# Two steps of an attention kernel written out anew: scores ahead of the values in front, exponentials ahead of weight roundings

## What is computed

```
x = x + tanh(g_x) * MHA(layernorm(x), ctx, ctx)        # 16 heads of 16
t = layernorm(x) * rsqrt(mean square + eps) * norm_w
probs = softmax(t @ gate_w.T); the two best of 8 experts, weights normalized
h1 = t @ w1.T + 2 * (t @ a1[e].T) @ b1[e].T            # rank 16 per expert
h3 = t @ w3.T + 2 * (t @ a3[e].T) @ b3[e].T
act = silu(h1) * h3
out_e = act @ w2.T + 2 * (act @ a2[e].T) @ b2[e].T
x = x + tanh(g_f) * sum over the two experts of weight * out_e
```

## Times and profile before

| | |
|---|---|
| three runs, median (lowest to highest) | 507.07 us (504.67 to 507.3) |
| the profiled execution, its own time | 509.6 us |
| its span, first to last instruction | 507.7 us |
| busy PE / DVE / ACT / POOL | 487.7 / 357.9 / 266.6 / 282.4 us |
| mean granted TensorE clock | 0.993 |

### The profile page before, as it was taken

The page is one execution under the profiler, slowest core; times in us unless marked ns, Lnnn a source line. Parts: engine busy times, 40 slices in busy tenths (PEclk is TensorE's granted clock), DMA queues, the critical chain, the costliest instruction groups (busy, mean ns, idle before and its releaser), DMA issues.

```text
span 507.7 us, 11754 instructions
## 1 busy us (share of the span) xinstructions
PE 487.7 (96%) x4350; PEld 456.2 (90%) x4350; DVE 357.9 (70%) x768; ACT 266.6 (53%) x584; POOL 282.4 (56%) x339
## 2 busy tenths in 40 slices
PE   7888999999999999999899999999999999999996
PEld 6657999999999999997789999899999999999994
DVE  6866777877878877888577869856486456854444
ACT  4456766666676777667666533443335333233331
POOL 5645666666666666561676536644386444854440
PEclk9989999999999999999989999999999999999999
DMA  7793786677777777553601000010000100001001
GB/s 199 180 289 93 216 214 153 157 182 190 189 179 180 180 176 169 120 111 57 204 10 17 1 0 1 1 34 0 1 0 2 34 1 1 0 2 34 0 1 32
DMA packets 51144, 45.83 MB, mean 90 GB/s; under 512 B 33935, under 2 KB 40115, under 8 KB 51088
## 3 DMA queue, kind: packets, MB, share of 16 engines
q1 hardware_dynamic: 41310, 23.18, 19.6%
q0 software_dynamic: 7504, 18.69, 14.1%
q10 hardware_dynamic: 2274, 3.21, 2.0%
HBM read 20.59 MB, written 6.66 MB: 54 GB/s over the span
## 4 chain that ended last, share of the span: by engine, by line
PE 84%; DVE 6%; DMA 5%; issue 2%; ACT 2%; POOL 1%; ACTq 0%; DVEq 0%
PE bank L1368 14%; PE bank L1223 7%; PE bank L1246 7%; PE bank L1372 7%; PE bank L1385 6%; PE bank L1420 6%; PE bank L1205 6%; PE bank L1259 6%; PE bank L1193 5%; PE bank L1400 4%; DMA QS<-crow 3%; PE bank L1292 3%; PE bank L1403 2%; PE bank L1180 2%; PE bank L1335 2%
## 5 line engine op out<-in xcount | busy, mean ns | idle before, releaser
L970 DVE TENSOR_REDUCE nmax<-bank 100x1 f32<-100x361 f32 x256 | 130.0, 529 | 38.4 <-PE bank L1223 33.4
L419 POOL TENSOR_TENSOR awl<-hb,awh 128x400 fp32r<-128x400 f32 x63 | 70.2, 1114 | 109.4 <-ACT awh L627 109.4
L529 ACT ACTIVATE pt<-bank 120x400 f32<-120x400 f32 (+1 forms) x192 | 90.3, 503 | 25.8 <-PE bank L1246 12.2
L627 ACT ACTIVATE awh<-hb 128x400 fp32r<-128x400 f32 x64 | 34.5, 539 | 119.0 <-DVE hb L906 118.7
L1223 PE MATMUL bank<-KS,QS 96*100 96x362 f32 x256 | 86.9, 358 | 5.2 <-DVE nmax L970 4.8
L899 DVE TENSOR_TENSOR hb<-sil,bank 128x400 f32<-128x400 f32 x64 | 36.5, 570 | 73.7 <-PE bank L1385 37.9
L1246 PE MATMUL bank<-QS,KS 97*120 97x200 f32 (+1 forms) x384 | 66.4, 271 | 1.6 <-ACT pt L529 1.0
L1246 PEld LDWEIGHTS bank<-QS,KS 97*120 97x120 f32 (+1 forms) x384 | 60.2, 184 | 2.8 <-DMA QS<-crow 1.7
L328 POOL TENSOR_TENSOR cth<-craw,cth 128x724 fp32r<-128x724 f32 x16 | 27.7, 1729 | 63.0 <-ACT cth L475 54.8
L1223 PEld LDWEIGHTS bank<-KS,QS 96*100 96x100 f32 x256 | 41.6, 167 | 12.8 <-DVE nmax L970 7.3
L333 POOL DMA_DIRECT2D QS<-q_dram x90 | 46.0, 519 | 0.4 <-issue 0.3
(11 more groups left out here) (221 smaller groups left out, 1116.3 us busy)
## 6 DMA issues: line engine op xcount, KB each, us to landing
KS<-kn SPq DMA_DIRECT2D x128, 90.5 KB, 3.3
KS<-kn POOLq DMA_DIRECT2D x64, 90.5 KB, 3.4
craw<-ctxT POOLq DMA_DIRECT2D x14, 361.0 KB, 4.9
QS<-q_dram POOLq DMA_DIRECT2D x92, 50.0 KB, 3.6
q_dram<-qn ACTq DMA_DIRECT2D x4, 400.0 KB, 4.1
o_dram<-on SPq DMA_DIRECT2D x16, 100.0 KB
xr<-o_dram SPq DMA_DIRECT2D x16, 100.0 KB
y<-xs SPq DMA_DIRECT2D x8, 200.0 KB
```

The source lines that it names most:

```text
L419: nc.gpsimd.tensor_tensor(awl[:, g % 2, slot], hb[:, slot], awh[:, g % 2, slot].bitcast(F32), ALU.subtract).then_inc(m["p_awl"], 1)
L529: nc.scalar.activation(pt[0:TW[t], u, :], pT[u % 3][0:TW[t], 0:CS], ACT.Exp, scale=float(DH) ** -0.5).then_inc(m["act_e"], 1)
L970: nc.vector.tensor_reduce(nmax[:, h // 8, pos % 8:pos % 8 + 1], pS[h % 2][0:S, 0:T], AX.X, ALU.max, negate=True).then_inc(m["dve_s"], 1)
```

## The change

Steps 14 and 15 get texts of their own (`late_step` and `last_step`) on PE, ACT and DVE. The rest of the attention is as it was, but for conditions that are always true now.

- PE: the first two scores of batch 15 stand ahead of the values of step 13, and units 0 to 2 of batch 15 ahead of the values of step 14. In step 15 the two halves of `u_proj` are apart, output turns and projection come earlier, `index_turn` stands behind all units, `weight_turn` behind the values.
- ACT: in step 14 exponentials come without a weight rounding between them; `row_copy` and `row_send` are parted by an exponential (before, the second followed the first at once in `row_out`). Pieces 0 to 2 are rounded between `tokens_high(0, 1)` and exponential 3 of batch 15, pieces 3 to 5 behind exponentials 9 and 10, piece 6 in tile 0. The four ACT instructions of `normed_x(1, ...)` go from step 15 to tiles 0 and 1.
- DVE: the same reductions, with the two `tokens_low`, the shares and the quotient at other places.
- POOL: the bias additions (L384) of batches 12 to 15 are all done in step 13; before, three of them stood in step 15. `second_u(0, ...)` waits for both `first_u`.
- `weight_turn(0)` waits for `d_ul` and no more for the masks.

```diff
-                for b in range(i - 2, B if i == B - 1 else i - 1):
+                for b in range(i - 2, B if i == B - 3 else i - 1):
...
             def second_u(n, low):
                 pool.wait_ge(m["p_md"], n + 1)
+                if n == 0:
+                    pool.wait_ge(m["d_u0"], 2)
...
+            def late_step():
...
+                row_copy(B - 2, 1)
+                expo(B - 2, 0)
+                row_send(B - 2, 1)
...
+                expo(B - 2, 11)
+                tokens_high(0, 1)
+                w_high(0)
+
+            def last_step():
+                expo(B - 1, 0)
+                expo(B - 1, 1)
+                w_high(1)
+                expo(B - 1, 2)
+                row_copy(B - 1, 1)
...
+                nc.scalar.activation(osb[:].rearrange("p q s -> p (q s)"), pO[:, 0:CS], ACT.Copy).then_inc(m["act_o"], 1)
+                row_send(B - 1, 1)
+                w_high(2)
...
+                w_high(3)
                 halves_of_weight(0)
                 w_high(4)
...
+                if g == 0:
+                    w_high(6)
...
-                if more and f < 2 and c:
+                if more and f < 2:
                     normed_x(c + 1, 2 * f)
                     normed_x(c + 1, 2 * f + 1)
...
+            def last_step():
+                gate(0)
+                o_turn(B - 1)
+                st_unit(B - 1, 3)
+                st_unit(B - 1, 4)
+                u_half(0, 0)
+                on_turn(B - 1)
+                st_unit(B - 1, 5)
+                st_unit(B - 1, 6)
+                st_unit(B - 1, 7)
+                u_half(0, 1)
+                st_unit(B - 1, 8)
+                st_unit(B - 1, 9)
+                st_unit(B - 1, 10)
+                y_proj(B - 1)
+                st_unit(B - 1, 11)
                 index_turn(0)
+                for u in range(UN):
+                    pv_unit(B - 1, u)
                 weight_turn(0)
```

More of the change, by code:

```diff
@@ L656, in body @@
                 expo(i, 5)
-                if has_k(i):
-                    wait(act, "pe_pv", i * UN)
-                    v_out(b, 0)
-                if i == B - 2:
-                    tokens_high(0, 0)
+                wait(act, "pe_pv", i * UN)
+                v_out(b, 0)
                 expo(i, 6)
@@ L720, in last_step @@
-                normed_x(1, 3)
+                expo(B - 1, 10)
+                w_high(5)
+                expo(B - 1, 11)
                 nc.scalar.activation(warm_s[:], nmr[:, 0:1], ACT.Silu).then_inc(m["silu_ok"], 1)
-            for i in range(0, B - 1):
+            for i in range(0, B - 2):
                 body(i)
-            last_step(B - 1)
+            late_step()
+            last_step()
             act.wait_ge(m["pe_pv"], B * UN)
@@ L1043, in body @@
                 head(i + 1, 8)
-                if i == B - 2:
-                    tokens_low(0, 0)
                 head(i + 1, 9)
@@ L1051, in body @@
                 head(i + 1, 12)
-                if i == B - 2:
-                    tokens_low(0, 1)
                 head(i + 1, 13)
@@ L1071, in body, with late_step @@
                     root(0, 6)
-            def last_step(i):
+            def late_step():
+                head(B - 1, 0)
+                head(B - 1, 1)
+                head(B - 1, 2)
+                head(B - 1, 3)
+                shares(B - 2)
+                head(B - 1, 4)
+                head(B - 1, 5)
+                quotient(B - 2)
+                head(B - 1, 6)
+                head(B - 1, 7)
+                head(B - 1, 8)
+                head(B - 1, 9)
+                tokens_low(0, 0)
+                head(B - 1, 10)
+                head(B - 1, 11)
+                turned_o(B - 2)
+                head(B - 1, 12)
+                head(B - 1, 13)
+                head(B - 1, 14)
+                first_sum(B - 2)
+                head(B - 1, 15)
+                tokens_low(0, 1)
+                variance(11)
+            def last_step():
+                shares(B - 1)
                 logits(0)
+                quotient(B - 1)
                 best_two(0)
-                shares(i)
-                quotient(i)
+                turned_o(B - 1)
                 u_low(0, 0)
@@ L1081, in last_step @@
                 masks(0)
-                turned_o(i)
                 first_u(0, 0)
                 first_u(0, 1)
-                first_sum(i)
+                first_sum(B - 1)
                 weights_of_two(0)
                 variance(13)
-            for i in range(0, B - 1):
+            for i in range(0, B - 2):
                 body(i)
-            last_step(B - 1)
+            late_step()
+            last_step()
             dve.wait_ge(m["tgf_ok"], 1)
@@ L1599, in body @@
                 s_head(i + 1, 15)
+                if i == B - 3:
+                    s_head(B - 1, 0)
+                    s_head(B - 1, 1)
                 for u in range(UN):
@@ new lines, in last_step @@
+            def last_step():
+                gate(0)
+                o_turn(B - 1)
[12 more added lines that the diff above has]
+                st_unit(B - 1, 11)
+                index_turn(0)
+                for u in range(UN):
+                    pv_unit(B - 1, u)
@@ L1622, in last_step @@
                 weight_turn(0)
-                y_proj(i)
-                for u in range(UN):
-                    pv_unit(i, u)
-            for i in range(0, B - 1):
+            for i in range(0, B - 2):
                 body(i)
-            last_step(B - 1)
+            late_step()
+            last_step()
             for g in range(NC * FT):
```

220 lines of the change are left out of this document (115 added, 105 removed).

## The result

The changed kernel takes **510.59 us** (median of 16 executions, 508.28 to 514.08); the kernel before took 507.97 us in 16 executions beside it (504.67 to 509.78). The ratio is 1.0057, 95% interval 1.0037 to 1.0078: slower by 0.57%; the medians themselves lie 2.6 us (0.52%) apart. It was wrong: the time is 4.0 us above the forecast, of which 0.9 us is the starting point (507.07 us was the median of three runs, 507.97 us is that of sixteen), 0.5 us the gain that did not come, and 2.6 us the loss that came in its place.

A forecast was written before the change was run, and what follows sets the result against it. PE's waits and low clock in steps 14 and 15 allowed at most 5.0 us; then the masks' chain binds. Step 14's 1.4 us was lost by the index turn; the entry left 0.5 us: 507.07 to 506.6 us, range 503.3 to 509.4.

The forecast's parts named there:

- Scores ahead of the values: Step 14: moving two scores of batch 15 makes PE 1.1 us late but comes to nothing, within 0.1 us.
- Step 14, 1.4 us: New order inside step 14: its values end at about 244.3 instead of 245.7, 1.4 us won.
- if later than 245: Sign of error: if step 14's values end later than 245, the walk of that step is wrong.
- Unit 6 waits for the send: Step 15, first half: PE reaches unit 6 at about 248.1 and waits 1.7 us for half 1's send.
- The send lands about 1.5 us earlier: Step 15: half 1's send, behind the weight loads, lands about 1.5 us earlier, at 249.9.
- Rival 4: Send lands 1.5 us later because batch 14's `on` store shares the engines; 1.0 survives: 507.6 us, chance 0.08.
- The index turn: End of step 15: index turn at about 252.8 against 253.00, so PE's gain is gone from the masks' chain.
- The entry: Feed-forward entry: masks' chain binds; PE waits for `first_u`, `second_u` and the projection copy; 1.7 us won, then 0.6 left.
- The four waits: PE waits between 248 and 269, from unit 6 to the projection copy: 1.7, 1.2, 1.8 and 0.7 us.
- The sum, "0.5 us won": At tile 2, beginning near 273.2 where it had begun at 273.6: 0.5 us won, bounds none and 5.0.
- Rival 3, the clock: PE's four waits lower the clock; two 3 us stretches behind tile 1 cost 3.0 us: 509.6 us, chance 0.10.

The follow-up runs named there:

- e1: Changed kernel run again, unedited, with a trace at full clock between step 13's projection and tile 3: 509.9 us, ratio 1.0057 to the kernel before.
- e12: Kernel before, unedited, one execution traced with the clock full from before step 13 to tile 3: 506.24 us.
- e8: Kernel before, unedited, one execution traced, with a low clock between step 13's projection and tile 3: 507.33 us.
- e2: Changed kernel plus 18, 9 and 8 filler transposes ahead of unit 6, the first delta and y_proj(16): 509.29 us, ratio 1.0028 to the kernel before.
- e3: Changed kernel with SP's six loads of second weight halves held until batch 15's half 1 send has landed: 506.44 us, ratio 0.9982 to the kernel before.
- e13: Changed kernel plus only the 18 filler transposes ahead of unit 6: 508.97 us, ratio 1.0034 to the kernel before.
- e9: Changed kernel with loads held, u's projection ahead of unit 5, index turn behind unit 7, roundings and tx moved: 504.59 us, ratio 0.9943 to the kernel before.
- e6: Changed kernel's new step 14 with the old order of step 15: 507.79 us, ratio 0.9999 to the kernel before.
- e11: Changed kernel, unedited, one execution traced: 509.03 us.

## Why the prediction was wrong

**Scores ahead of the values: right.** PE 1.1 us late was forecast; the values start 2.59 us behind the projection (226.81 and 229.40 above), where it was 1.28: 1.3 us.

**Step 14, 1.4 us: right in kind, 0.55 us too much.** The forecast was the end of the values, 244.3 for 245.7, or 15.2 of the ruler for 16.6. They end at 15.75: 0.85 us won. That the gate comes 1.5 us earlier, 15.8 for 17.3, is this and the 0.7 us of units 0 to 2, which stood between the two and now stand in front. The bound "if later than 245" (15.9) was just kept. The send is issued at 16.4, 0.7 us earlier than before and not 1.3, and PE comes to unit 6 at 19.7, not 19.0.

**Unit 6 waits for the send: right in kind, 1.3 us too early.** The wait of 1.7 us was forecast; it is 1.9 to 2.5 us. The forecast put unit 6 at 249.9, which is 20.8 of the ruler; e1 has 22.1. "The send lands about 1.5 us earlier" was argued from the store of `on`, the loads behind it and the send behind the loads. SP's queue of the changed kernel:

```profile
234.57 0.28 SPq L287 DMA_DIRECT2D o_dram<-on  x1
238.25 0.28 SPq L294 DMA_DIRECT2D xr<-o_dram  x1
...
241.54 0.94 SPq L301 DMA_DIRECT2D w<-w2T  x1
245.42 0.31 SPq L287 DMA_DIRECT2D o_dram<-on  x1
```

The store is at 7.76 of the ruler, 1.3 us earlier than before's 9.07, but `xr` only at 11.44 against 12.46: the loads came 1.0 us earlier, not 1.5. By as much came the send, from 23.1 (e12, where PE waits for it) to 22.1. The other 0.8 us are the landing before, which I took as 251.4, or 22.3, from a trace in which PE waited there for an exponential and did not show it; where PE does wait for it, it is 22.75 (e8) and 23.1. It moves from one execution to the next, in the changed kernel from 21.6 to 22.3. Rival 4, the store of the next `on` (the last row) sharing the engines, was given 0.08: that store now comes 2.2 us behind the send's issue, and in e12 it came 4.0 behind. But from issue to unit 6 it is 5.2 to 5.8 us in the seven traces of the changed kernel and 5.6 and 6.0 in e8 and e12, so the store has not made the send slower. From the issue of the first load to unit 6 it is 9.9 to 10.5 us in the seven and 9.9 and 10.3 in the two: the send goes out with the tail of the loads, in either order.

Here the Trainium skill had been put against the row (DMA: Bandwidth & Descriptors, "Queues, rings and completion order"). No trace agrees with a send that takes its turn: in all seven of the changed kernel its packets moved 3.3 to 5.6 us behind the issue.

**The index turn, "252.8 against 253.00 before": failed.** 252.8 is 23.7 of the ruler; it came at 25.4 in e1, 26.5 as profiled. From unit 6 on the forecast's 2.9 us of PE work became 3.3 at full clock, and 4.8 to 4.9 where the clock fell; in the old order the index turn stood 0.8 us behind unit 6 (e12). So the masks' chain, said to be no later, is 1.2 to 1.7 us later than before's 23.9 even at full clock. **This is the step that failed**, the late send and the longer walk behind it, 1.4 us together at the least (25.1 for 23.7); and all but 0.3 us of the slowdown at full clock is there already.

**The entry: right in every wait, again with sizes.** `first_u` sat out POOL as foreseen in e1 (1.69 us, beneath b3's low part); in the changed kernel as profiled, where the masks came later, the first takes 0.99 us. Then `md` starts just behind the first `first_u`, and the second just before `md` ends, and each is the longer for it. The changed kernel as profiled, DVE:

```profile
254.27 1.17 DVE L896 TENSOR_SCALAR mk<-bank,erow 128x400 f32<-128x400 f32 x2 [2.32 <-PE bank L1384]
255.48 0.99 DVE L902 TENSOR_TENSOR uth<-uTh,mk 128x800 fp32r<-128x800 f32 x1
256.38 1.83 DVE L902 TENSOR_TENSOR utl<-uTl,mk 128x800 fp32r<-128x800 f32 x1
...
264.31 2.19 DVE L918 TENSOR_TENSOR hb<-hb,wbT 128x400 f32<-128x400 f32 x1
266.53 1.30 DVE L924 TENSOR_TENSOR aws<-hb 128x400 f32<-128x400 f32 x1
267.76 0.35 DVE L968 COPY ot<-bank 128x200 f32<-128x200 f32 x1
```

and POOL:

```profile
255.52 1.85 POOL L406 TENSOR_TENSOR md<-mk 128x400 f32<-128x400 f32 x1 [0.84 <-DVE mk L896]
258.36 1.92 POOL L416 TENSOR_TENSOR uth<-uTh,md 128x800 fp32r<-128x800 f32 x1 [0.99 <-DVE utl L902]
260.23 1.90 POOL L416 TENSOR_TENSOR utl<-uTl,md 128x800 fp32r<-128x800 f32 x1
262.08 1.63 POOL L402 TENSOR_TENSOR a2l<-a,a2h 128x512 fp32r<-128x512 f32 x1
263.67 2.39 POOL L402 TENSOR_TENSOR w2l<-w,w2h 128x1024 fp32r<-128x1024 f32 x1
```

The weighting of slot 1 takes 2.19 us, since it starts beneath POOL's w2 (2.39 us), and the copy for the projection ends at 268.1: the last wait. With the same delays the changed order's way from the index turn to tile 3 is 28.0 us in every trace at full clock, also in e2, e3 and e13. The four waits were forecast as 1.7, 1.2, 1.8 and 0.7 us; e1 has 2.36, 0.94, 1.10 and 0.99.

**The sum, "0.5 us won": failed, in its base.** On the ruler the forecast for tile 2 (273.2) is 44.1; measured at full clock 45.3. That is a miss of 1.2 us, as much as unit 6's. The other part is on the side of before. I wrote that "the clock takes about 1.7 us more" in its step 15 and counted the stretch at 0.50 as part of the old order's time, then walked the new order with a full clock. Tile 2 of before was at 44.5 in that trace and is at 43.5 in e12: the old order's time was taken 1.0 us too long, by the clock of one execution. Forecast 44.1 less 44.5, −0.4 (the text rounds to 0.5 won); measured at equal clock 45.3 less 43.5, +1.8. The difference of 2.2 us is 1.2 from the walk and 1.0 from the base. The note that the profiled execution stood 2.5 us above the median was the warning; it was used to shift the sum, not to ask whether the stretch at 0.50 was typical.

**Rival 3, the clock: open.** It had 0.10. Expected were stretches behind tile 1; in seven traces none was seen there while PE had work. In three a low stretch of some 3.5 us lies directly behind unit 6. What the timed executions show, all of either kernel pooled: the kernel before has a mean clock of 0.9958 (97 executions, median 507.6 us), the changed one 0.9930 (33, 510.3 us). Among those at 0.996 or more the medians are 506.7 (49) and 508.5 (9): **1.8 us, the same as the ruler's 1.7**. So the order, forecast at −0.5, is +1.8, with the clock or without. The remaining 0.8 of 2.6 us goes with a lower clock: 15 of 33 executions lie below 0.993, with 7 of 97 before. That the change causes this by the wait at unit 6 is argued, from e2 and e13, whose fillers raise the mean clock, and from e3. The traces of the unedited kernels do not locate it: six of ten have low stretches in front of both steps, and a low clock at the end of the span counts in the mean and costs nothing.

**What stays open.** No execution of the changed kernel above 511.5 us was traced, so where its clock falls in those isn't seen, and how much of 0.8 us the wait at unit 6 costs isn't either. Nor is it shown why in some executions the clock falls behind a wait of 2.0 us and in others, as e1 with 2.36 us, not.

## What to carry to other kernels

Before work is moved from behind a short transfer's landing to ahead of it or the other way, find when it lands in the trace, and what covers it: half a projection moved over unit 6 helped uncover a send that stood behind 2.3 MB of loads, and the chain behind it (index turn, masks, masked products) carried that on to the end. A gain on the busiest engine counts only at the point where the next chain starts: here 1.5 us at the gate were worth nothing until the index turn came earlier too (e3, e9). And a single profiled execution can hold a clock stretch that its kernel does not always have: take two or three, lay them over a point that both kernels share, and make the sum against the one without it.

## What the runs showed of the hardware

- **A send on one queue behind loads on another.** 16 packets on q10, issued by ACT, moved 3.3 to 5.6 us behind the issue with SP's 2.3 MB of loads in flight, 1.1 to 1.6 us with the loads held (e3). Holding the loads, which are issued 6.4 us later on the ruler in e3, made no engine wait for them; `xr`, behind them in the same queue, came late enough in e9 for a wait of 0.38 us.
- **The start of the stretch moves by 4 us.** Step 13's projection starts between 226.5 and 230.8 us in the traces, also of the same kernel (226.5 to 229.0 in the changed one), and later work doesn't make up for it. Differences of one profile against another below that say nothing unless taken from a common point.
- **A low clock can follow a wait of PE and cost as much again.** In the three traces where the clock fell behind the 1.9 to 2.5 us wait at unit 6, the first product comes 1.0 to 2.0 us later than in the traces of the same kernel without (29.9 to 30.4 against 28.4 to 28.9), of which 0.3 to 1.3 us reach tile 3. 18 transposes that compute nothing, in the same place, raise the mean clock of twelve executions from 0.9938 to 0.9967. The old order has a low stretch too in two of its three traces, without a wait of that length before it (0.3 to 0.8 us).
- **Lost clock and lost time are not the same.** The kernel before as profiled is at half clock for 3.5 us in step 15; it loses 1.5 us by the first product and 1.0 us by tile 3, the rest being taken up by waits that are there anyway. e6, at half clock for 6.9 us, takes 1.7 us more from the index turn to tile 3 than e12. A low clock in the last 3 us, where PE has no work (e11), costs nothing and still lowers the mean.
